# First attention: VectorE forms the keys' low half a quarter later, and TensorE transposes the values ahead of the value sums

## What is computed

```python
x = L0_attn_inputs                                   # (8, 512, 256)
xn = _layernorm(x, axis=-1)
s = _L0_attn_ref(xn, L0_attn_W_qkv, L0_attn_W_out)   # the part that the change touches
g = _silu(_L0_ffn_ref(xn, ...))
x = x + s * g
...                                                  # the second layer

def _L0_attn_ref(inputs, W_qkv, W_out):              # 32 query heads, 16 key/value heads of 64
    qkv = inputs @ W_qkv
    q, k, v = ...                                    # k and v repeated for 2 query heads each
    scores = einsum('bhqd,bhkd->bhqk', q, k) / sqrt(64) + ALIBI_SLOPES * rel
    scores = where(causal, scores, -inf)
    out = einsum('bhqk,bhkd->bhqd', softmax(scores), v)
    return out @ W_out
```

## Time and profile before

| | before |
|---|---|
| median of 3 timed runs | 3618.19 us (3616.73 to 3621.49) |
| the profiled execution | 3613.86 us, span from first to last instruction 3612.1 us |
| mean granted TensorE clock | 0.962 |
| busy over the span | PE 92%, PEld 70%, DVE 67%, ACT 60%, POOL 34% |
| the 128 steps of the first attention | from about 83 to 1646 us of the span |

### The profile page before, as it was taken

How to read it: one execution, slowest core, us unless ns; L and a number is a source line. 1 busy time by engine, 2 the same in 40 slices (tenths; PEclk the granted TensorE clock), 3 DMA queues, 4 the chain that set the end, 5 groups by cost and what they waited for, 6 DMA issues and landing times. The chain is left out here.

```text
span 3612.1 us, 67403 instructions
## 1 busy us (share of the span) xinstructions
PE 3329.0 (92%) x19106; PEld 2537.6 (70%) x19106; DVE 2434.8 (67%) x6978; ACT 2168.2 (60%) x5051; POOL 1212.5 (34%) x1841
## 2 busy tenths in 40 slices
PE   3999999999999999997999997979999974999995
PEld 2777777777777777776888885546666654888885
DVE  4777777777777777776666664546666635666665
ACT  2777777777777777775555554315665640555553
POOL 6333333333333333333333331023313102244442
PEclk9999999999999999999999998979999976999998
DMA  2222222222222222224434332110111123554545
GB/s 68 43 55 51 57 51 54 54 51 57 51 55 53 51 52 45 56 52 157 137 116 143 128 125 79 47 52 22 28 27 30 28 90 104 151 144 121 143 123 158
DMA packets 175532, 280.43 MB, mean 78 GB/s; under 512 B 32434, under 2 KB 117170, under 8 KB 175410
## 3 DMA queue, kind: packets, MB, share of 16 engines
q1 hardware_dynamic: 160818, 258.94, 25.1%
q0 software_dynamic: 14592, 19.93, 3.4%
HBM read 159.79 MB, written 41.16 MB: 56 GB/s over the span
## 5 line engine op out<-in xcount | busy, mean ns | idle before, releaser
L706 POOL TENSOR_SCALAR at_p<-at_p,at_recip 128x128 f32<-128x128 f32 (+3 forms) x1028 | 533.7, 532 | 983.7 <-DVE at_recip L845 983.7
L756 ACT ACTIVATE at_p<-at_p,at_nmax 128x128 f32<-128x128 f32 (+3 forms) x1030 | 575.9, 559 | 290.5 <-DVE at_nmax L839 287.2
L839 DVE CUSTOM_DVE_ANT_0 at_p<-at_s_ps,at_bias 128x128 f32<-128x128 f32 (+3 forms) x1030 | 493.9, 480 | 154.5 <-PE at_s_ps L954 154.5
L961 PE MATMUL at_t_ps<-ident,at_p 128*128 128x128 f32 x2560 | 459.5, 277 | 0.4 <-POOL at_p L706 0.4
L953 PE MATMUL at_s_ps<-at_k_twice,at_q 128*128 128x128 f32 (+3 forms) x1030 | 386.9, 376 | 8.1 <-DVE at_nmax L839 1.2
L1778 DVE CUSTOM_DVE_ANT_0 aa_a_ps<-aa_a_ps,aa_hidden 128x128 f32<-128x128 f32 (+3 forms) x512 | 247.3, 507 | 173.7 <-PE aa_a_ps L1942 170.4
L954 PE MATMUL at_s_ps<-at_k_twice,at_q 128*128 128x128 f32 (+3 forms) x1030 | 332.0, 322 | 0.0
L961 PEld LDWEIGHTS at_t_ps<-ident,at_p 128*128 128x128 f32 x2560 | 295.1, 140 | 46.2 <-DVE at_pT L852 30.0
L971 PE MATMUL at_o_ps<-at_pT,at_v 128*64 128x512 f32 (+3 forms) x2064 | 306.3, 439 | 0.0
L1678 ACT ACTIVATE aa_pT<-aa_b_ps 128x512 f32<-128x512 f32 (+1 forms) x384 | 196.5, 529 | 176.3 <-PE aa_b_ps L1960 173.5
L971 PEld LDWEIGHTS at_o_ps<-at_pT,at_v 128*64 128x64 f32 x2064 | 136.7, 136 | 175.8 <-issue 156.9
(11 more groups left out here) (314 smaller groups left out, 8484.0 us busy)
## 6 DMA issues: line engine op xcount, KB each, us to landing
at_k_twice<-at_k_parts SPq DMA_DIRECT2D x260, 256.0 KB, 3.7
nw_w_raw<-in_w_all_dram SPq DMA_DIRECT2D x52, 1024.0 KB, 7.5
w_raw<-in_w_dram SPq DMA_DIRECT2D x57, 768.0 KB, 5.8
nw_xh<-xh_dram SPq DMA_DIRECT2D x10, 512.0 KB, 4.3
nw_xl<-xl_dram SPq DMA_DIRECT2D x10, 512.0 KB, 4.9
at_w_raw<-in_w_heads_dram SPq DMA_DIRECT2D x18, 256.0 KB, 4.4
nw_x<-in_x_dram SPq DMA_DIRECT2D x9, 512.0 KB, 6.9
x_dram<-nw_x SPq DMA_DIRECT2D x9, 512.0 KB, 3.0
```

The source lines that it names most:

```text
L706: pool.tensor_scalar(p, p, recip[:, u:u + 1], 1.0, ALU.mult, ALU.mult).then_inc(scaled, 1)
L756: act.activation(p_sb[:, u, 0:N], p_sb[:, u, 0:N], ACT.Exp, bias=nmax[:, u:u + 1], scale=-1.0, accum_out=total[:, u:u + 1]).then_inc(exped, 1)
L839: dve.tensor_tensor_reduce(out=p_sb[:, u, 0:N], in0=s_ps[u % 2][:, 0:N], in1=bias[:, u % 2, S - N:S], scale=1.0, scalar=BIG, op0=ALU.add, ...
L961: ins = pe.transpose(t_ps[u % 2][:, k * P:k * P + P], p_sb[:, u, k * P:k * P + P], ident[:])
```

## The change

`k_rest` moves, in VectorE's order, from the end of quarter 1 to the end of quarter 2, behind both masks of that quarter and ahead of the first `add_out`. `turn_v` moves, in TensorE's order, from behind the value sums to ahead of them. All waits keep their numbers, since the order of what counts up `proj_out` and `proj` among the users of each count stays.

```diff
@@ head_attention_phase, VectorE's body
                     if qt == 1:
                         values(v_count(t + 1), 1 - par)
                         rest_o(t, 1 - par)
+                    if qt == 2:
                         k_rest(t + 2, par)
                     if qt == 3:
                         add_out(t + (-1), 1 - par, b_before, 1)
@@ head_attention_phase, TensorE's body
                     if qt == 0:
+                        turn_v(t + 1, 1 - par, v_count(t + 1) + (-2))
                         weigh(t + (-1), 1 - par)
-                        turn_v(t + 1, 1 - par, v_count(t + 1) + (-2))
```

## The result

The changed kernel takes 3580.51 us (median of 4, 3577.51 to 3582.6) against 3617.46 for the kernel before (median of 4, 3615.97 to 3621.49). The ratio is 0.9895, 95% interval 0.9883 to 0.9907. The forecast was 3581.

What follows compares the result with a forecast made beforehand. The prediction took TensorE to bound the first attention phase, losing 0.29 us per step to late VectorE work. Over 128 steps that is 37 us, 3618.2 − 37 = 3581 us with the swap at nothing; range 3573 to 3602.

Steps and rivals of the forecast that it cites:

- What bounds the phase: First attention stretch: TensorE bounds it, busy 1559 of 1570 us, with 0.29 us a step lost inside busy time.
- The four starts of quarter 3: TensorE, last output projection to next score: 0.945 us without waits instead of 1.23, so 0.285 lost per step.
- The mask's new start: VectorE, first mask of quarter 2: starts 0.19 us after its scores end, about 603.78, 1.5 us earlier.
- rival A: Quarter 3: only half comes back, one wait returning under another name; gain 19 us, 3599 us; chance 0.08.
- Spare: Quarter 3: mask and probability copy both ready over 1 us before TensorE wants them, at 605.72 and 606.07.
- that addition as covered: VectorE's output addition behind `k_rest` starts at 605.60, not 606.51; the projection awaiting it, then at 607.21, is covered.
- The keys: SyncE's two key copies start 0.3 us later, land near 609.4, are first read at 625; cost nothing.
- The swap: Value transposes ahead of value sums on TensorE: three shape changes at today's sizes, no gain; upper bound 0.15 us a step.
- rival C: At the swap, two releases not passed in advance cost 0.36 us per step; slower, 3627 us; chance 0.05.
- rival B: Next head's first score: TensorE arrives 0.29 us earlier and waits at `q_rest`, losing the gain; 3618 us; chance 0.05.
- Sum: Whole kernel: 0.29 us x 128 steps = 37 us, from 3618.2 to 3581 us; step 11.90 us.

Runs made afterwards that it cites:

- k_early_release: Kernel before, both orders kept; ScalarE signals the keys' high half before copying the values and `k_rest` waits for that; 3580.85 us, ratio 0.9897.
- ballast3: Changed kernel plus three 128x512 additions with unused results on VectorE ahead of the first mask of quarter 2; 3640.58 us, ratio 1.0074.
- swap_only: Kernel before with only the value transposes moved ahead of the value sums, `k_rest` left in quarter 1; 3618.15 us, ratio 1.0003.
- q_early_no_swap: Changed kernel with `q_rest` ahead of the second mask of quarter 0 and value transposes behind the value sums as before; 3564.89 us, ratio 0.9861.
- q_early: Changed kernel with `q_rest` ahead of the second mask of quarter 0 instead of behind it; 3564.04 us, ratio 0.9856.
- k_only: Kernel before with only `k_rest` moved, value transposes still behind the value sums; 3578.44 us, ratio 0.9888.

## Why the prediction was right

- **What bounds the phase.** That the loss sat inside TensorE's busy time held: 11 us by the busy share, 37 by the starts, 37 measured (3617.46 − 3580.51). The Trainium skill, "Perfetto Trace Analysis", section "Identifying the Most-Contended Engine", calls the matmul busy share no good measure of how near TensorE is to its limit. These traces agree: the share was 99.3% before and 99.4% after.
- **The four starts of quarter 3.** Forecast 0.945, measured 0.95. The loss of 0.285 was sized from rows without a wait, and so included what no wait row shows: the slower pass and the slower transposes behind a gap. One choice in it was right without a reason given: for the first pass the prediction took 0.18, the second pass of the other half. The first pass of that half takes 0.25 (606.72 to 606.97); with it the loss would have been 0.215 a step, 27.5 us and 3591. That the 0.18 held goes with the 512-column matmul ahead of the pass, as in the quarter 0 rows above.
- **The mask's new start.** Forecast 0.19 behind its scores' end: 603.11 + 0.28 = 603.39, start 603.58. `k_rest` 1.21 later forecast, 1.22 measured. Both of TensorE's waits for VectorE went, so rival A did not come about.
- **Spare.** "Over 1 us to spare" was right for the mask and the copy: k_early_release leaves the mask 0.95 us later than the changed kernel (1.42 less 0.47) and loses nothing. But the place as a whole has less. Most of what ballast3 loses, with the mask 1.32 us later, it loses at the output addition of quarter 3. The prediction named that addition as covered and did not say that it is the nearest.
- **The keys.** The prediction lets them be read first at 625. By the kernel's order (the first score of quarter 1 of step t is of step t + 1) it is one step earlier, at 613.03. The cover behind the landing near 609.4 was then 3.6 us and not 15. It still cost nothing: in the changed kernel the two copies start at 605.50, with 3.7 us to landing 609.2, and the score is at 612.56.
- **The swap.** Forecast nothing, in today's sizes for the changes of shape. swap_only says so with the wait for `q_rest` as cover, q_early_no_swap without it. Value transposes to sums take 0.38 from the first transpose (609.75 to 610.13), as value transposes to scores did. Sums to score take 2.30 from the first sum, as sums to value transposes do (604.43 to 606.73 in q_early_no_swap). The feared double stop of the sequencer (rival C) did not happen: the transposes of the values start 0.21 behind the last transpose of probabilities, and swap_only is no slower than the kernel before.
- **`q_rest` (rival B).** Its 0.12 us stayed as forecast and took none of the gain, because its chain starts from a score. q_early removed it and measured it: 0.12 a step, 3580.5 to 3564.0.
- **Sum.** 0.29 x 128 = 37. The step fell from 12.19 to 11.90. That the time came out within 0.5 us of the forecast is in part luck: the runs of the changed kernel spread over 5 us, and the medians of the kernel before lie between 3615.29 and 3618.19.

Not tried: what the key copies would cost if they were not covered. ballast3 comes nearest: the copies start at 603.01 there, with 3.7 us to landing 606.7, and the score that reads them is at 609.20.

## What to carry to other kernels

Read a stall on a saturated engine from the distance between starts, against the same work a little further on that runs undisturbed; the busy share hides it, and the wait rows show only a part. Compare only with work that has the same kind of instruction ahead of it: here the same pass took 0.17 behind 512 columns and 0.26 behind transposes, with no wait in either. Before moving an instruction out of the way, ask for what moment its successor is wanted: here 0.58 of the 1.37 us of idle time gave all of the gain, and a mask 0.71 us later than in the changed kernel cost 0.02 us a step, one 1.32 us later 0.47. When two edits travel together, time each alone: the swap of value transposes and value sums did nothing.

## What the runs showed of the hardware

- The distance across a change of shape between matmuls did not depend on the shape that came next. Behind a 128-column transpose (128*128) it was 0.20 to sums (128*64, 610.02 to 610.22) and 0.21 to value transposes (64*128, 609.54 to 609.75). From the first of four value transposes it was 0.38 to sums and 0.38 to scores, so 0.14 behind the last (0.38 less 0.24). That this is the time in which the matmul ahead drains fits these numbers and was not tested.
- A matmul that starts behind a gap of 0.05 us makes its successor 0.10 late as well (605.77 to 606.05 in the earlier trace rows, 605.53 to 605.70 without the gap), and transposes behind a gap take 0.42 for four, not 0.35. The rows of the weight loads go with it. Where the score waits, its load starts with it; where it does not, the load starts 0.24 us ahead of it. One row of the kernel before and one of the changed kernel:

```profile
605.77 0.19 PEld L953 LDWEIGHTS at_s_ps<-at_k_twice,at_q 128*128 128x128 f32 x1 [0.32 <-DVE at_nmax L839]
```

```profile
605.29 0.19 PEld L954 LDWEIGHTS at_s_ps<-at_k_twice,at_q 128*128 128x128 f32 x1
```

- What the change doesn't touch varies by 7 us between profiled executions. From the last value transposes to the end of the span, in the four kernels without the swap, are 1975.3 us before (3612.1 − 1636.8), 1982.2 in k_only, 1979.1 in k_early_release and 1975.7 in q_early_no_swap. The pair of profiled executions alone would have given 34 us (3613.86 − 3579.9).
